# Where on one DMA queue the copy of x to the output goes out: two pieces early and six among the Toeplitz loads, instead of six early and two late

## The chip, the cores and the metric

The kernel runs on one core of one Trainium2 chip. The metric is the time of one execution in microseconds; the kernel before takes 540.82 us, the median of three runs (539.96 to 542.36). A core has five engines, each with its own instruction stream: TensorE (PE in the profile) multiplies matrices, VectorE (DVE), ScalarE (ACT) and GpSimd (POOL) work elementwise, and SyncE (SP) here does nothing but wait on semaphores and issue DMAs. DMAs that SP issues are one queue (q1), those of ACT another (q10), those of POOL a third (q0); all three are served by the same 16 DMA engines.

## The reference

x has the shape 32 x 64 x 1024 (batch, channel, time), all float32. The layer convolves each channel over time with a kernel of its own, then runs a mixture of experts over the 2048 (channel, batch) rows and adds its result to x:

```python
kernel = _get_kernel(log_dt, C, log_A_real, A_imag, Lq)      # 64 channels x 1024 taps
y = irfft(rfft(u*mask) * rfft(kernel))[..., :Lq]             # causal convolution over time
y = (y + u_m * D[:, None]) * mask
...
logits = y_rows @ gate_w.T ; top 2 of 16 experts, weights w
h = silu(y_rows @ g.T) * (y_rows @ u.T)                      # 112 wide per expert
out = einsum('bei,hei,be->bh', h, d_r, w)
return x + out.reshape(x.shape)
```

The "x +" of the last line is what this change is about: the output tensor has to hold a copy of x before the experts' results are added into it.

## The kernel before

**The convolution.** The 64 channels are worked in 16 groups of 4 (`G` = 16, `HG` = 4). A channel's convolution is a product with a Toeplitz matrix. For group g, TensorE makes the taps (`products`, k_bank), VectorE copies them out (`kernel_rows`, k_sb), SP stores them to a DRAM tensor `k_rows` (L303, 16 KB), and SP then reads them back as a Toeplitz matrix: 128 partitions, each one a row of 1024 taps that starts one element further (L314 for groups 0 and 1, four loads of 512 KB with a semaphore each; L317 for the others, one load of 2 MB). I call these the tap store and the Toeplitz load of a group. Also needed is the group's part of x with time on the partitions (`x_time`, L308, 512 KB). TensorE then runs 8 matmuls of up to 256 columns for each channel (L988; the trace counts 16 records for them), VectorE masks them (L742) and transposes blocks (L751), and ACT stores the group's rows to DRAM (`y_rows`, L525, four stores of 128 KB).

**What orders SP's queue.** `toep` and `u_t` have two buffers each, picked by g % 2. In each turn of its loop over g SP does this, in order: wait until the taps of g are in k_sb (`k_added`); issue the tap store; wait until the convolution of group g-2 has ended (`conv_done`); issue the load of x_time; wait until the tap store has landed (`k_stored`); issue the Toeplitz load of g. The next turn begins with the tap store of g+1. So the tap store of g+1 always stands behind the Toeplitz load of g in the same queue, and the Toeplitz load of g+1 is not issued before that store has landed.

**The copy of x.** `copy_x(q)` (L281 to L284) copies rows 256q to 256q+255 of x, 1 MB, from DRAM to DRAM, straight into `out`. There are eight pieces. Six are issued at the start, before the tap store of group 0; two are issued after the loop over g and after the weights of the first four experts (L296, L297). Only POOL waits for the pieces: `pool.wait_ge(x_copied, 8 * 16)`, ahead of the first scatter into `out`.

**The experts.** Rows are sorted by expert in tiles of 128. For each tile POOL gathers rows (L442), TensorE transposes them (L1105), multiplies with the gate and up weights (L1097) and the down weights (L1115), and POOL adds the weighted result into `out` by a scatter that accumulates (L458). Experts beyond the first four have their weights loaded as the earlier ones are used up.

Of the kernel before, what the change touches and what calls it, by code (L numbers as in the profile page):

```python
# [40 lines left out]
def build(nc, x_time, x_rows, lengths, params, skip, gate_t, gu_t, d_t, out):  # L41
# [4 lines left out]
    with ctx:  # L46
# [224 lines left out]
        @block.sync  # L271
        def _(sp):
            sp.dma_start(par[:, :, :], params).then_inc(par_in, 16)
            sp.dma_start(skip_row[:, :], skip).then_inc(par_in, 16)
            sp.dma_start(len_i[:, :], lengths.partition_broadcast(P)).then_inc(len_in, 16)
            sp.dma_start(gate_w[:, :, :], gate_t).then_inc(gate_in, 16)

            for g in range(2):
                sp.dma_start(u_t[:, g, :, :], x_time[:, g * HG:(g + 1) * HG, :]).then_inc(u_in[g], 16)

            def copy_x(q):  # L281

                part = slice(q * (TOK // 8), (q + 1) * (TOK // 8))
                sp.dma_start(out[part, :], x_rows[part, :]).then_inc(x_copied, 16)  # L284

            sp.wait_ge(ys_cleared, 1)
            sp.dma_start(out[TOK:, :], ys[:, 0, :]).then_inc(spare_out, 16)
            sp.wait_ge(zero_made, 1)
            sp.dma_start(k_rows.ap()[:, 0:P - 1], zero[:, 0:P - 1]).then_inc(pads_out, 16)
            for q in range(6):  # L290
                copy_x(q)
            sp.wait_ge(pads_out, 16)

            def load_expert(e):
                s = e % WB
                sp.dma_start(w_gu[:, s * C * GU:(s + 1) * C * GU], gu_t[e]).then_inc(w_in[s], 16)  # L296
                sp.dma_start(w_d[:, s * L:(s + 1) * L], d_t[e]).then_inc(w_in[s], 16)  # L297

            for g in range(G):
                p, i = g % 2, g // 2  # L300

                sp.wait_ge(k_added, g + 1)
                sp.dma_start(bass.AP(k_rows, g * HG * KROW + P - 1, [[LO, LO], [KROW, HG], [1, LO]]),  # L303
                             k_sb[:, p, :, :]).then_inc(k_stored[p], 16)

                if g >= 2:
                    sp.wait_ge(conv_done, (g - 1) * HG)
                    sp.dma_start(u_t[:, p, :, :], x_time[:, g * HG:(g + 1) * HG, :]).then_inc(u_in[p], 16)  # L308

                sp.wait_ge(k_stored[p], 16 * (i + 1))  # L310
                if g < 2:

                    for h in range(HG):
                        sp.dma_start(toep[:, p, h, :], bass.AP(k_rows, (g * HG + h) * KROW, [[1, P], [1, L]])  # L314
                                     ).then_inc(toep_first[p][h], 16)
                else:
                    sp.dma_start(toep[:, p, :, :], bass.AP(k_rows, g * HG * KROW, [[1, P], [KROW, HG], [1, L]])  # L317
                                 ).then_inc(toep_in[p], 16)

            for e in range(WB):  # L320
                load_expert(e)
            for q in range(6, 8):
                copy_x(q)

            for e in range(WB):
                sp.wait_ge(w_in[e % WB], 32)
                sp.sem_inc(weights_ready, 1)
            sp.wait_ge(ends_made, 1)
            sp.wait_ge(lists_made, 1)
            for e in range(WB, E):  # L330

                end = sp.value_load(ends_i[0:1, e - WB:e - WB + 1], min_val=1, max_val=MT)
                sp.wait_ge(down_done, end)
                load_expert(e)
                sp.wait_ge(w_in[e % WB], 32 * (e // WB + 1))
                sp.sem_inc(weights_ready, 1)
# [851 lines left out]
```

## Time and profile before

| | |
|---|---|
| median of three runs | 540.82 us (539.96 to 542.36) |
| the profiled execution | 542.34 us |
| its span | 540.5 us |
| PE busy | 457.0 us, 85% |
| weight loads (PEld) busy | 391.3 us, 72% |
| DVE, ACT, POOL busy | 38%, 18%, 32% |
| DMA moved | 119.94 MB, mean 222 GB/s |
| SP's queue q1 | 73.49 MB, 41.4% of 16 engines' span |

The execution lasts 542.34 us, of which the profile's span holds 540.5. The kernel has three stages: a prologue to about 33 us, in which parameters are worked out while the DMA engines copy; the convolution, to about 220 us; then routing (to about 250 us) and the experts. The busy shares are means over all three, so the question for each stage is which wait ends last in it. The chain of waits (part 4 of the page, and the chain in order of time) follows the work that ended last back to what released it. The queue's own instructions are seen in SP's timeline; a row of it gives the start and length of the issue, not of the transfer.

### The profile page before, as it was taken

To read this page: it belongs to the slowest core of one execution; us is meant where nothing else is said; L and a number is where in the kernel's file an instruction comes from. 1 tells how busy PE (TensorE), PEld (TensorE's weight loads), DVE (VectorE), ACT (ScalarE), POOL (GpSimd) and SP (SyncE) were. 2 spreads that over 40 slices of the span, in tenths; PEclk is the share of its full clock that TensorE was granted. 3 is DMA by queue.
4 is the path that set the end of the run, shared out by engine and by line. 5 is a ranking of instruction groups with operands and counts; after the bars stand their busy time and mean duration, and the time that the engine had idled before them with its cause. 6 is when DMAs were issued, how large, how long until landed. Compare 5 with 4: busy or idle time off the path is not lost.

```text
span 540.5 us, 9417 instructions
## 1 busy us (share of the span) xinstructions
PE 457.0 (85%) x2867; PEld 391.3 (72%) x2868; DVE 204.6 (38%) x560; ACT 99.1 (18%) x230; POOL 172.1 (32%) x215
## 2 busy tenths in 40 slices
PE   0479799999998998958899889899899798899881
PEld 0469798988888988857777667677677576677660
DVE  6914334533334325494233233232333223333321
ACT  3930000000000000200122122221222122222210
POOL 5244222233221100063144332353343334344331
PEclk9989899999999999968899999999999989999996
DMA  8958978788888889922278878989887968868553
GB/s 297 312 159 274 310 244 274 274 266 279 285 289 256 290 269 333 333 106 77 75 216 215 213 182 247 249 232 258 231 180 225 274 185 183 241 134 176 83 80 69
DMA packets 39466, 119.94 MB, mean 222 GB/s; under 512 B 7442, under 2 KB 15890, under 8 KB 39314
## 3 DMA queue, kind: packets, MB, share of 16 engines
q1 hardware_dynamic: 18418, 73.49, 41.4%
q0 software_dynamic: 11808, 37.76, 31.6%
q10 hardware_dynamic: 9216, 8.39, 4.6%
q8 instruction: 13, 0.21, 0.2%
q14 instruction: 11, 0.09, 0.1%
HBM read 94.68 MB, written 38.57 MB: 247 GB/s over the span
## 4 chain that ended last, share of the span: by engine, by line
PE 44%; DMA 35%; issue 8%; DVE 8%; POOL 2%; ACT 0%; POOLq 0%; ACTq 0%; DVEq 0%; SPq 0%
PE conv_ps L988 18%; DMA out<-od,to_row 12%; PE conv_ps L1097 11%; DMA ys<-y_rows,from_row 10%; DMA arena<-k_rows 7%; PE conv_ps L1115 7%; DMA k_rows<-k_sb 6%; PE turn_ps L1105 4%; PE conv_ps L1083 1%; PE turn_ps L999 1%; DVE tmp L637 1%; POOL out L458 1%; DVE od L933 1%; POOL arena L430 1%; DVE mask_t L786 1%
## 5 line engine op out<-in xcount | busy, mean ns | idle before, releaser
L988 PE MATMUL conv_ps<-arena 128*128 128x256 f32 (+7 forms) x1024 | 158.4, 311 | 16.5 <-DMA arena<-k_rows 9.6
L988 PEld LDWEIGHTS conv_ps<-arena 128*128 128x128 f32 x1024 | 150.3, 194 | 24.6 <-issue 13.5
L1097 PE MATMUL conv_ps<-w_gu,ys_t 128*128 x656 | 135.9, 361 | 13.8 <-issue 11.5
L1097 PEld LDWEIGHTS conv_ps<-w_gu,ys_t 128*128 128x128 f32 x656 | 122.3, 192 | 33.3 <-issue 32.9
L458 POOL DMA_INDIRECT out<-od,to_row x40 | 63.5, 1587 | 132.3 <-DMA out<-od,to_row 70.1
L1115 PE MATMUL conv_ps<-w_d,hid_t 112*128 x160 | 76.9, 603 | 0.0
L742 DVE TENSOR_TENSOR arena<-conv_ps,mask_t 128x256 f32<-128x256 f32 x64 | 26.9, 423 | 97.9 <-PE conv_ps L988 96.8
L442 POOL DMA_INDIRECT ys<-y_rows,from_row x42 | 44.5, 1059 | 46.4 <-PE turn_ps L1105 34.3
L933 DVE TENSOR_SCALAR od<-conv_ps,weight_now 128x512 f32<-128x512 f32 x40 | 30.0, 751 | 72.2 <-DMA out<-od,to_row 47.1
L1105 PE MATMUL turn_ps<-ident,ys 128*128 128x128 f32 x336 | 45.8, 281 | 13.3 <-DMA ys<-y_rows,from_row 13.3
L1105 PEld LDWEIGHTS turn_ps<-ident,ys 128*128 128x128 f32 x336 | 39.7, 144 | 18.5 <-DMA ys<-y_rows,from_row 17.0
L913 DVE TENSOR_TENSOR hid<-silu,conv_ps 128x112 f32<-128x112 f32 x41 | 11.1, 271 | 91.7 <-ACT silu L576 91.7
L387 POOL TENSOR_TENSOR am<-wave,cs_re 128x128 f32<-128x128 f32 x16 | 6.4, 399 | 117.1 <-ACT wave L519 109.6
L1115 PEld LDWEIGHTS conv_ps<-w_d,hid_t 112*128 112x128 f32 x160 | 27.7, 193 | 20.3 <-issue 19.8
L584 ACT ACTIVATE od<-conv_ps,weight_now 128x512 f32<-128x512 f32 x40 | 27.5, 687 | 75.1 <-DMA out<-od,to_row 48.2
L905 DVE COPY ys_t<-turn_ps 128x512 f32<-128x512 f32 x42 | 29.1, 692 | 27.7 <-PE turn_ps L1105 27.4
L569 ACT COPY ys_t<-turn_ps 128x512 f32<-128x512 f32 x42 | 24.6, 585 | 66.1 <-PE turn_ps L1105 65.5
L576 ACT ACTIVATE silu<-conv_ps 128x112 f32<-128x112 f32 x41 | 10.8, 262 | 96.2 <-PE conv_ps L1097 96.1
L519 ACT ACTIVATE wave<-angle 128x384 f32<-128x384 f32 x16 | 8.2, 521 | 106.7 <-DVE angle L687 106.7
L1039 PE MATMUL turn_ps<-ones 128*128 128x128 f32 x50 | 8.3, 341 | 20.7 <-DVE cs_im L722 20.7
L430 POOL TENSOR_TENSOR arena<-arena,token_no 128x384 f32<-128x384 f32 (+1 forms) x5 | 7.2, 1449 | 54.4 <-DVE arena L867 54.4
L1039 PEld LDWEIGHTS turn_ps<-ones 128*128 128x128 f32 x50 | 7.9, 251 | 20.4 <-issue 20.4
(151 smaller groups left out, 309.8 us busy)
## 6 DMA issues: line engine op xcount, KB each, us to landing
arena<-k_rows SPq DMA_DIRECT2D x14, 2048.0 KB, 10.9
w_gu<-gu_t SPq DMA_DIRECT2D x16, 896.0 KB
arena<-x_time SPq DMA_DIRECT2D x16, 512.0 KB, 4.0
y_rows<-y_blk ACTq DMA_DIRECT2D x64, 128.0 KB, 7.4
w_d<-d_t SPq DMA_DIRECT2D x16, 448.0 KB
arena<-k_rows SPq DMA_DIRECT2D x8, 512.0 KB, 6.0
ys<-y_rows,from_row POOLq DMA_INDIRECT x42
out<-od,to_row POOLq DMA_INDIRECT x40
```

Source lines behind the costliest of these rows:

```text
L442: nc.gpsimd.indirect_dma_start(out=ys[:, t % 2, :], out_offset=None, in_=y_rows, in_offset=bass.IndirectOffsetOnAxis(ap=from_row[:, t:t + ...
L458: nc.gpsimd.indirect_dma_start(out=out, out_offset=bass.IndirectOffsetOnAxis(ap=to_row[:, t:t + 1], axis=0), in_=od[:, t % 2, :], in_offse ...
L569: nc.scalar.copy(ys_t[:, p, 0:C // 2, :], ytr_ps[:, 0:L // 2].rearrange("p (c n) -> p c n", n=P)).then_inc(yst_act, 1)
L584: nc.scalar.mul(od[:, p, 0:L // 2], down_ps[:, 0, :], weight_now[:, p:p + 1]).then_inc(od_act, 1)
L742: nc.vector.tensor_tensor(y_t[:, p, h, :, :], conv_ps[:, h, 0:C * B].rearrange("p (c b) -> p c b", c=C), mask_t[:, :, :], ALU.mult).then_i ...
L905: nc.vector.tensor_copy(ys_t[:, p, C // 2:, :], ytr_ps[:, L // 2:].rearrange("p (c n) -> p c n", n=P)).then_inc(yst_dve, 1)
L933: nc.vector.tensor_scalar(od[:, p, L // 2:], down_ps[:, 1, :], weight_now[:, p:p + 1], None, ALU.mult, ALU.bypass).then_inc(od_dve, 1)
L988: last = nc.tensor.matmul(conv_ps[:, h, d * B:C * B], toep[:, p, h, d * P:(d + 1) * P], u_t[:, p, h, 0:(C - d) * B], start=(d == 0), stop= ...
L1039: nc.tensor.matmul(bank, ones[:, :], ones[:, :], start=True, stop=True)
L1097: last = nc.tensor.matmul(gu_ps, ys_t[:, p, c, :], w_gu[:, bass.ds(buf * (C * GU) + c * GU, GU)], start=(c == 0), stop=(c == C - 1))
L1105: last = nc.tensor.transpose(ytr_ps[:, c * P:(c + 1) * P], ys[:, p, c * P:(c + 1) * P], ident[:, :])
L1115: last = nc.tensor.matmul(down_ps[:, n, :], hid_t[:, p, :], w_d[:, bass.ds(buf * L + n * (L // 2), L // 2)], start=True, stop=True)
```

## The change

Two pieces of the copy are issued at the start instead of six. The other six are issued one at a time in the loop over g, each right behind the Toeplitz loads of groups 1, 3, 5, 7, 9 and 11. None is left behind the expert weights. All other instructions are the same, on all engines.

```diff
@@ -287,7 +287,7 @@
             sp.dma_start(out[TOK:, :], ys[:, 0, :]).then_inc(spare_out, 16)
             sp.wait_ge(zero_made, 1)
             sp.dma_start(k_rows.ap()[:, 0:P - 1], zero[:, 0:P - 1]).then_inc(pads_out, 16)
-            for q in range(6):
+            for q in range(2):
                 copy_x(q)
             sp.wait_ge(pads_out, 16)
 
@@ -316,11 +316,11 @@
                 else:
                     sp.dma_start(toep[:, p, :, :], bass.AP(k_rows, g * HG * KROW, [[1, P], [KROW, HG], [1, L]])
                                  ).then_inc(toep_in[p], 16)
+                if g in (1, 3, 5, 7, 9, 11):
+                    copy_x((1, 3, 5, 7, 9, 11).index(g) + 2)
 
             for e in range(WB):
                 load_expert(e)
-            for q in range(6, 8):
-                copy_x(q)
```

What SP issues from the start to the load of group 2, before and then after (`out<-x_rows` is a piece of the copy, `k_rows<-k_sb` a tap store, `arena<-k_rows` a Toeplitz load, `arena<-x_time` the group's part of x):

```order
L284 DMA out<-x_rows 16x16384 x6
L303 DMA k_rows<-k_sb 32x4x32
L314 DMA arena<-k_rows 128x1024 x4
L303 DMA k_rows<-k_sb 32x4x32
L314 DMA arena<-k_rows 128x1024 x4
L303 DMA k_rows<-k_sb 32x4x32
L308 DMA arena<-x_time 128x1024
L317 DMA arena<-k_rows 128x4x1024
```

```order
L284 DMA out<-x_rows 16x16384 x2
L303 DMA k_rows<-k_sb 32x4x32
L314 DMA arena<-k_rows 128x1024 x4
L303 DMA k_rows<-k_sb 32x4x32
L314 DMA arena<-k_rows 128x1024 x4
L284 DMA out<-x_rows 16x16384
L303 DMA k_rows<-k_sb 32x4x32
L308 DMA arena<-x_time 128x1024
L317 DMA arena<-k_rows 128x4x1024
```

Four pieces have left the place ahead of the first tap store, and one now stands between the Toeplitz loads of group 1 and the tap store of group 2.

Further on in the loop, SP's stream around the Toeplitz load of group 3, as a piece of the difference:

```order
 L308 DMA arena<-x_time 128x1024
 L317 DMA arena<-k_rows 128x4x1024
+L284 DMA out<-x_rows 16x16384
 L303 DMA k_rows<-k_sb 32x4x32
 L308 DMA arena<-x_time 128x1024
```

One piece stands ahead of the tap store of group 4; four more such places follow, ahead of the tap stores of groups 6, 8, 10 and 12.

## Rows read from the trace of the kernel before

**Rows 1.** The page: busy tenths in 40 slices of 13.5 us, and chain shares.

```profile
PEclk9989899999999999968899999999999989999996
DMA  8958978788888889922278878989887968868553
PE 44%; DMA 35%; issue 8%; DVE 8%; POOL 2%; ACT 0%; POOLq 0%; ACTq 0%; DVEq 0%; SPq 0%
```

**Rows 2.** Chain in order of time, prologue and first groups: start, us, what.

```profile
24.20 4.90 DMA k_rows<-k_sb
29.11 4.20 DMA arena<-k_rows
33.44 4.02 PE conv_ps L988 x16
...
46.25 2.46 PE conv_ps L988 x16
...
56.89 2.89 issue
59.78 3.95 PE conv_ps L988 x16
```

**Rows 3.** Chain in order of time, the middle of the convolution.

```profile
105.05 0.92 issue
...
108.11 9.29 DMA k_rows<-k_sb
117.42 11.03 DMA arena<-k_rows
```

**Rows 4.** SP's timeline, its DMA issues: start, us, line, DMA, count.

```profile
4.96 4.94 SPq L284 DMA_DIRECT2D out<-x_rows  x6
24.20 0.35 SPq L303 DMA_DIRECT2D k_rows<-k_sb  x1
...
38.36 0.32 SPq L303 DMA_DIRECT2D k_rows<-k_sb  x1
40.28 1.75 SPq L314 DMA_DIRECT2D arena<-k_rows  x4
...
71.67 0.33 SPq L308 DMA_DIRECT2D arena<-x_time  x1
72.05 0.43 SPq L317 DMA_DIRECT2D arena<-k_rows  x1
...
115.69 0.33 SPq L308 DMA_DIRECT2D arena<-x_time  x1
117.42 0.37 SPq L317 DMA_DIRECT2D arena<-k_rows  x1
...
197.03 0.37 SPq L317 DMA_DIRECT2D arena<-k_rows  x1
```

**Rows 5.** Windows: stretch, length, engines' busy us, PE clock, DMA share, GB/s.

```profile
11.00:14.00 3.00, 0.00 (x0) 0.00 (x0) 2.71 (x6) 2.95 (x9) 2.33 (x5) 1.00 1.02 350
14.00:17.00 3.00, 0.00 (x0) 0.00 (x0) 2.62 (x12) 2.99 (x9) 0.00 (x0) 1.00 1.05 371
17.00:20.00 3.00, 0.00 (x0) 0.00 (x0) 2.76 (x17) 3.00 (x14) 0.00 (x0) 1.00 1.07 350
20.00:23.00 3.00, 2.09 (x9) 1.82 (x10) 2.93 (x13) 3.00 (x14) 2.17 (x6) 1.00 1.04 328
23.00:26.00 3.00, 3.00 (x19) 2.94 (x20) 2.90 (x7) 3.00 (x14) 0.69 (x1) 1.00 1.14 355
26.00:29.00 3.00, 3.00 (x28) 3.00 (x27) 0.95 (x3) 2.98 (x13) 0.00 (x0) 1.00 0.04 6
72.00:197.00 125.00, 117.17 (x985) 110.75 (x985) 51.80 (x120) 8.15 (x21) 27.05 (x58) 1.00 0.86 279
```

**Rows 6.** Timeline of PE, ACT and POOL where the convolution begins.

```profile
23.53 6.30 PE L1039 MATMUL turn_ps<-ones 128*128 128x128 f32 x42
32.35 0.45 POOL L396 TENSOR_TENSOR am<-am,arena 128x128 f32<-128x128 f32 x1
37.39 0.44 PE L980 MATMUL k_bank<-bm,am 128*32 128x32 f32 x8
```

**Rows 7.** Timeline of PE, first and last channels of groups: start, us, idle time before.

```profile
105.36 2.48 PE L988 MATMUL conv_ps<-arena 128*128 128x256 f32 x16 [0.70 <-DMA arena<-k_rows]
108.35 4.79 PE L988 MATMUL conv_ps<-arena 128*128 128x256 f32 x32
113.19 2.46 PE L988 MATMUL conv_ps<-arena 128*128 128x256 f32 x16
117.09 2.48 PE L988 MATMUL conv_ps<-arena 128*128 128x256 f32 x16 [1.07 <-DMA arena<-k_rows]
...
209.00 2.46 PE L988 MATMUL conv_ps<-arena 128*128 128x256 f32 x16 [2.10 <-issue]
```

**Rows 8.** Chain in order of time behind the convolution, to the first gather.

```profile
240.16 7.81 PE conv_ps L1083 x48
...
249.65 5.38 DMA ys<-y_rows,from_row
```

**Rows 9.** Windows around the two late pieces, columns as in rows 5.

```profile
203.00:233.00 30.00, 24.79 (x210) 23.47 (x208) 17.03 (x90) 3.83 (x7) 0.00 (x0) 1.00 1.03 332
229.00:240.00 11.00, 5.50 (x33) 5.09 (x31) 10.63 (x24) 0.53 (x2) 5.97 (x6) 0.75 0.35 138
```

**Rows 10.** Tile x_rows, issue to landing of the eight pieces; tile out, POOL's scatters.

```profile
DMA to landing us min/median/max: 8.7/16.6/30.2
...
L458 POOL DMA_INDIRECT out<-od,to_row x40: 1552/1587/1631, 273.0 to 530.6; - x40
```

## The prediction

> **What bounds the kernel now.** I read the page first. Its slices of 13.5 us show the DMA engines busy for seven to nine tenths through the whole convolution, slices 4 to 15, and the chain that ended last is PE for 44% and DMA for 35% [rows 1]. So in that stage two things are near their limit, and the question is which wait ends last in each group.
>
> The chain in order of time answers it. In the middle of the convolution it goes from a tap store, 9.29 us from issue to landing, straight to a Toeplitz load, 11.03 us [rows 3]. The same 16 KB store takes 40.28 - 38.36 = 1.92 us when the queue ahead of it is empty [rows 4]. So the other 7.4 us are the Toeplitz load of the group before, which stands ahead of it in SP's queue. PE started on that load's data at 117.09 [rows 7] and the store landed by 117.42, when SP issued the next load [rows 4]. Each group therefore costs one full pass of the queue: Toeplitz load, tap store behind it, receipt, next Toeplitz load. From 72.05 to 197.03 there are 11 groups [rows 4], 11.36 us each.
>
> PE is close behind but not the limit. A group's matmuls run from 105.36 to 113.19 + 2.46 = 115.65; PE's next group starts at 117.09, after 1.07 us without work that ended with the Toeplitz load [rows 7]. The last group starts at 209.00 after 2.10 us of idling [rows 7]. A group keeps PE busy for some 10.7 us, the 117.17 us busy over 11 groups [rows 5]. SP issues x_time at 115.69, when group g-2 has ended, 1.7 us ahead of the Toeplitz load [rows 4]; that loop has 1.7 us of slack.
>
> In the prologue the pieces of the copy run from before 11 us to 26 us, and from 26 to 29 the DMA engines carry next to nothing, 6 GB/s [rows 5]. The tap store of group 0 was issued at 24.20 and took 4.90 us [rows 2].
>
> **The start.** Two pieces instead of six end some 12 us earlier, at about 14 us, far ahead of the store at 24.20. The store then takes its 1.92 us instead of 4.90: 2.98 us less. It lands at 26.1, and the first Toeplitz channel 4.20 us later [rows 2], at 30.3. PE's filler matmuls end at 23.53 + 6.30 = 29.8 [rows 6], so its idle time falls from 3.6 us to about 0.6. The first 16 matmuls took 4.02 us after the long idling, where a warm group's take 2.46 [rows 2]; I expect 2.46, another 1.5 us. What is late next is POOL: the factors of group 1 are ready at 32.35 + 0.45 = 32.8, and PE's products of group 1, now at 37.39, come at 30.4 + 2.5 = 32.9 [rows 6]. That just fits. Sum for the start: -4.5 us. Bounds: -3.0 if the first channel stays slow, -4.5 if not.
>
> **The six moved pieces.** A piece is 256 rows of 4 KB, 1.05 MB. In the five windows from 11 to 26 us the queue moves 350, 371, 350, 328 and 355 GB/s for 3 us each [rows 5], 5.26 MB in 15 us, so 3.0 us a piece. In the changed program each stands behind a Toeplitz load and ahead of the next tap store. The store waits for the queue to drain, as its 9.29 us show, so its landing and the next Toeplitz load move by the whole piece. Nothing hides it: the engines' idle time of the stage, 14% [rows 5], 1.6 us of each 11.36, lies behind the tap store, while its receipt comes back and the next load is issued, and a piece ahead of the store can't slide there. Six times 3.0 is +18.0 us. The issue itself, 4.94 / 6 = 0.8 us on SP [rows 4], is over before the load ahead of it has drained. An upper bound for a piece comes from the mean rate of the stage, 279 GB/s [rows 5], at which 1.05 MB take 3.8 us, 22.5 us for six.
>
> Two small terms go the other way. The Toeplitz load of group 4 was issued at 72.05 only because group 2's matmuls ended late: x_time went out at 71.67 [rows 4], since PE had idled 2.89 us and run a slow first channel of 3.95 us [rows 2]. With a piece in front of that load, PE is no longer what it waits for; I take 0.5 us off. And as every pair of groups gets 3 us longer, x_time and the y_rows stores are issued earlier against the Toeplitz load and fill more of the idle 1.6 us. That lies between 0 and 6 x 1.6 = 9.6 us. I take 2.0, close to nothing, because x_time already goes out 1.7 us ahead and its 0.5 MB take about that long.
>
> PE waits for each even group some 3 us longer. Behind its waiting matmul are the gates and products of that turn, and VectorE and ACT wait for these; all of them have two groups of room. After 2.89 us of idling PE's first channel took 3.95 us instead of 2.46 [rows 2]. So 1.5 us more for PE every second group; a pair then takes it 2 x 10.7 + 1.5 = 22.9 us against 2 x 11.36 + 3.0 = 25.7 us of queue. It stays hidden.
>
> **The two late pieces.** They leave the stretch 203 to 233 us, where DMA runs at 332 GB/s [rows 9]. Nothing on the chain waits for them: it goes through routing to the 48 table matmuls at 240.16 and the gather at 249.65, which takes 5.38 us [rows 8], and by 229 to 240 the DMA rate has fallen to 138 GB/s [rows 9]. POOL needs the copy first at its scatter at 273.0 [rows 10]. Gain 0. The new last piece, behind group 11, lands by about 165 us, so no wait is added there either. The weights of the first experts still follow the last Toeplitz load and move with it.
>
> **Sum.** -4.5 + 18.0 - 0.5 - 2.0 = +11.0 us. The profiled execution took 542.34 us (span 540.5), so 553.3 for it. It lay 1.5 us above the median of the runs; against the median that is 551.8, say 552.
>
> **A rule that speaks against the change even more.** The copy moved 351 GB/s in the prologue, which counts each byte once; read and written it is some 700 GB/s at the DRAM [rows 5]. The Trainium skill, page "HBM Reference", section "Specifications (TRN2)", puts a core's effective share of the memory's bandwidth at about 358 GB/s. By that, 2.1 MB read and written for a piece would take an estimated 5.9 us, and six of them 35 us. This case's trace doesn't agree for a copy that runs by itself, at 3.0 us a piece.
>
> **The rivals.**
>
> 1. The pieces are hidden (faster). If the store did not wait for them, because the engines took it past the piece or spread the piece over their idle time, six pieces would need 18 us of a stage in which 14% of 125 us, 17.5 us, are idle [rows 5]. Cost about 0, and the start's 4.5 us stay: 536.3 us. For it: the room is just enough. Against it: the 9.29 us of the store show that it is served behind what is ahead of it. It decides as soon as the tap store behind a piece lands no later than one without. 7%.
>
> 2. Part of it is hidden. The idle time is filled to between half and all: 4.8 to 9.6 us back instead of 2, so +3.4 to +8.2, 544 to 549 us, centre 546. 13%.
>
> 3. Reading and writing at once is the limit beside other traffic. In the stage the memory already serves 279 GB/s, and a piece has to be read and written. At 279 GB/s for both ways together a piece costs 2 x 3.8 = 7.5 us, six 45, with the start +40: 581 us. The windows of 700 GB/s both ways speak against it, though there nothing else ran. 2%.
>
> 4. PE's slow clock comes onto the path, or the pieces cost the 3.8 us. If each of six idle times brings 1.5 us that are not hidden, +9 on top of 11: 561 us; with 3.8 us a piece and nothing filled, 22.5 - 3.0 = +19.5, 560 us. For it: 2.89 us of idling did bring the slow channel. Against: the 2.8 us of room for a pair. 9%.
>
> **How the numbers follow.** The forecast, +7 to +16 us, 548 to 557, gets 69%. The range takes in the second rival and the upper bound of the fourth, 544 to 560, and leaves out the hidden copy and the memory limit. Within 0.5% (2.7 us, about what a measurement of this kernel can tell from no change) lies the edge between rivals 1 and 2, 5%; faster by more 6%; slower by more 89%.
>
> **What would show it.** In the changed profile: the tap store of group 0 lands about 2 us after its issue, and the first matmul on Toeplitz data starts near 30.5 us. SP's Toeplitz issues alternate, about 14.2 us from odd to even groups and 11.3 from even to odd, up to group 12, then 11.4 steadily. PE waits some 3 us for the Toeplitz load of each even group. The last group's matmuls start near 220 us instead of 209.00, and what follows keeps its length. The forecast is wrong if the steps from odd to even groups stay near 11.4 us, or if the copy costs over 4 us a piece.

## The result and the profile after

The changed kernel takes 548.12 us (median of four, 546.38 to 553.12) against 540.39 of the kernel before in the same series: ratio 1.0152, 95% interval 1.008 to 1.0225. It is slower by some 8 us, as forecast in sign; the forecast was 552.0, the range 544 to 560. Some executions of every kernel run in a slower state with a lower clock: the ratios leave them out, the medians given here and below are of all executions.

The profiled execution is a long one, 553.12 us with a span of 551.3. The page's slices, columns as in [rows 1], show the emptied slice 2 (13.8 to 27.6 us) and a granted clock that fell to 0.6 and 0.7 in slices 5 and 9 (0.8 and 0.9 before), and more mildly in slice 12:

```profile
PEclk9999699979989999978799999999999989999996
DMA  8079968878999889901377879989887978767753
```

SP's timeline of the changed kernel answers to [rows 4]:

```profile
24.21 0.35 SPq L303 DMA_DIRECT2D k_rows<-k_sb  x1
25.76 1.77 SPq L314 DMA_DIRECT2D arena<-k_rows  x4
...
36.04 1.75 SPq L314 DMA_DIRECT2D arena<-k_rows  x4
37.83 0.62 SPq L284 DMA_DIRECT2D out<-x_rows  x1
...
47.63 0.38 SPq L317 DMA_DIRECT2D arena<-k_rows  x1
...
57.36 0.37 SPq L317 DMA_DIRECT2D arena<-k_rows  x1
57.77 0.56 SPq L284 DMA_DIRECT2D out<-x_rows  x1
...
72.09 0.34 SPq L308 DMA_DIRECT2D arena<-x_time  x1
72.48 0.43 SPq L317 DMA_DIRECT2D arena<-k_rows  x1
...
84.64 0.37 SPq L317 DMA_DIRECT2D arena<-k_rows  x1
...
98.37 0.37 SPq L317 DMA_DIRECT2D arena<-k_rows  x1
...
109.07 0.37 SPq L317 DMA_DIRECT2D arena<-k_rows  x1
...
123.30 0.34 SPq L308 DMA_DIRECT2D arena<-x_time  x1
123.69 0.43 SPq L317 DMA_DIRECT2D arena<-k_rows  x1
...
180.96 0.43 SPq L317 DMA_DIRECT2D arena<-k_rows  x1
```

The first store lands 1.55 us after its issue. I call the time from one group's Toeplitz issue to the next group's a step. The steps alternate, as foreseen: from group 5 (84.64) to 6 it is 13.7 us, from 6 to 7 10.7. Over the six of each kind from group 1 to 13, the steps from odd to even groups average 13.5 us (before: 11.1) and those from even to odd 10.6 (before: 11.4). At groups 4 and 8 something else shows: x_time went out 0.39 us ahead of the Toeplitz load. There SP was not waiting for the tap store but for PE, which had to end groups 2 and 6 (at group 4 the trace of before shows the same, 71.67 and 72.05 in [rows 4]). PE's timeline shows why (start, length, idle time ahead; the columns of [rows 7]):

```profile
57.25 4.66 PE L988 MATMUL conv_ps<-arena 128*128 128x256 f32 x16 [4.45 <-issue]
62.85 6.69 PE L988 MATMUL conv_ps<-arena 128*128 128x256 f32 x32
...
108.43 4.69 PE L988 MATMUL conv_ps<-arena 128*128 128x256 f32 x16 [2.32 <-DMA arena<-k_rows]
114.06 6.68 PE L988 MATMUL conv_ps<-arena 128*128 128x256 f32 x32
...
158.06 3.86 PE L988 MATMUL conv_ps<-arena 128*128 128x256 f32 x16 [2.64 <-DMA arena<-k_rows]
162.64 4.79 PE L988 MATMUL conv_ps<-arena 128*128 128x256 f32 x32
```

Behind its waits PE ran at 0.50 of its clock, the lower of its two levels (1.2 instead of 2.4 GHz), in the windows from 57 to 66 and from 108 to 117 us, and groups 2 and 6 took some 4.5 us longer each than the groups behind them. Group 10 lost 1.4 us.

The last group's channels start at 214.84 instead of 209.00 [rows 7], +5.8 us; the first gather comes at 256.24 instead of 249.65 [rows 8]. From there to the end of the span it is 295.1 us against 290.9, 4.2 us that come behind the loop.

### The profile page after: what moved, and what is told of

Its sections match the earlier page's. It is cut to its first block, busy times and chain, and to the rows that moved or that the text cites. A ratio compares the mean times of both kernels' runs of the same rounds, so it can differ in the third digit from the quotient of the medians.

```text
span 551.3 us, 9417 instructions
## 1 busy us (share of the span) xinstructions
PE 465.9 (85%) x2867; PEld 396.4 (72%) x2868; DVE 205.1 (37%) x560; ACT 99.2 (18%) x230; POOL 172.4 (31%) x215
## 4 chain that ended last, share of the span: by engine, by line
DMA 39%; PE 38%; issue 7%; DVE 5%; ACT 4%; POOL 3%; POOLq 1%; ACTq 0%; DVEq 0%; SPq 0%
DMA out<-od,to_row 23%; PE conv_ps L988 22%; DMA ys<-y_rows,from_row 8%; PE conv_ps L1097 6%; PE conv_ps L1115 4%; DMA k_rows<-k_sb 4%; DMA arena<-k_rows 4%; ACT arena L503 3%; PE turn_ps L1105 3%; PE turn_ps L999 1%; PE conv_ps L1083 1%; DVE od L933 1%; POOL ys L442 1%; POOL out L458 1%; POOL arena L430 1%
## 5 line engine op out<-in xcount | busy, mean ns | idle before, releaser
L988 PE MATMUL conv_ps<-arena 128*128 128x256 f32 (+7 forms) x1024 | 165.0, 320 | 14.8 <-issue 7.3
L988 PEld LDWEIGHTS conv_ps<-arena 128*128 128x128 f32 x1024 | 156.3, 201 | 23.4 <-issue 17.9
L1115 PE MATMUL conv_ps<-w_d,hid_t 112*128 x160 | 78.2, 612 | 0.0
L913 DVE TENSOR_TENSOR hid<-silu,conv_ps 128x112 f32<-128x112 f32 x41 | 11.1, 272 | 90.8 <-ACT silu L576 90.8
L1115 PEld LDWEIGHTS conv_ps<-w_d,hid_t 112*128 112x128 f32 x160 | 27.6, 193 | 20.9 <-issue 19.7
L576 ACT ACTIVATE silu<-conv_ps 128x112 f32<-128x112 f32 x41 | 10.8, 263 | 95.5 <-PE conv_ps L1097 95.3
## 6 DMA issues: line engine op xcount, KB each, us to landing
y_rows<-y_blk ACTq DMA_DIRECT2D x64, 128.0 KB, 7.0
w_d<-d_t SPq DMA_DIRECT2D x16, 448.0 KB, 11.7
```

What stands on the lines that cost most here:

```text
L988: last = nc.tensor.matmul(conv_ps[:, h, d * B:C * B], toep[:, p, h, d * P:(d + 1) * P], u_t[:, p, h, 0:(C - d) * B], start=(d == 0), stop= ...
L1115: last = nc.tensor.matmul(down_ps[:, n, :], hid_t[:, p, :], w_d[:, bass.ds(buf * L + n * (L // 2), L // 2)], start=True, stop=True)
```

## The experiments

All were timed in five rounds beside the kernel before: e1 to e4 together, e5 to e8, e9 and e10, e11 and e12. For each I also give, from its trace, the time from the Toeplitz issue of group 1 to that of group 13, "the twelve steps". It holds the six pieces and leaves out the start. In the first trace of before it is 175.01 (the row below) less 40.28 [rows 4], 134.7 us; in that of the changed kernel 180.96 - 36.04 = 144.9.

```profile
175.01 0.37 SPq L317 DMA_DIRECT2D arena<-k_rows  x1
```

| kernel | ratio to before (95%) | median us, all executions | twelve steps |
|---|---|---|---|
| changed | 1.0152 (1.008 to 1.0225) | 548.12 | 144.9 |
| e6 changed, again | 1.019 (1.0119 to 1.0261) | 545.31 | 139.5 |
| e5 before, again | 1.0005 (0.9956 to 1.0053) | 538.23 | 129.2 |
| e1 five early, three late | 0.9957 (0.9923 to 0.999) | 534.52 | 129.2 |
| e7 two early, six late | 0.9926 (0.988 to 0.9973) | 533.14 | 132.1 |
| e12 the same, PE warmed | 0.9914 (0.9874 to 0.9955) | 531.85 | 128.0 |
| e4 pieces behind tap stores | 1.003 (0.9989 to 1.0072) | 539.52 | 135.9 |
| e3 fillers at even groups | 1.0159 (1.0118 to 1.02) | 545.19 | 141.7 |
| e8 pieces on ACT's queue | 1.0151 (1.008 to 1.0222) | 545.70 | 144.2 |
| e9 six extra pieces | 1.0149 (1.0073 to 1.0225) | 547.26 | 143.6 |
| e2 twelve halves | 1.0241 (1.0197 to 1.0284) | 550.47 | 144.4 |
| e10 three pairs | 1.0258 (1.0206 to 1.031) | 550.58 | 152.1 |
| e11 three pairs, PE warmed | 1.014 (1.0087 to 1.0193) | 543.14 | 138.5 |

**e1, five pieces early, three late.**

```diff
-            for q in range(6):
+            for q in range(5):
...
-            for q in range(6, 8):
+            for q in range(5, 8):
```

> Five pieces go out at the start and three behind the expert weights; none in the loop over the groups. Theory A (the start's gain is real, the moved pieces are the loss): the fifth piece ends at about 23 us, before the tap store of group 0 at 24.2, so the store lands in under 2 us, the convolution starts near 29.8 us and ends 3 to 4.5 us earlier than in the kernel before, at 215.5 to 217 us; 536 to 537.5 us in all. Theory B (what starts earlier is lost again at a later wait): the convolution ends at 219 to 220 us and the time is 540 to 541.

Measured: the first Toeplitz load was issued at 25.71 (before: 29.11 [rows 2] and 28.55), the ratio is 0.9957. The start's gain is real, some 2.3 us by the ratio (0.5 to 4.1 by its interval). The trace ended its convolution at 208.3, earlier than A said, because its steps from group 6 on were 10.3 to 10.9 us long and not 11.4. That called for a second trace of before (e5).

**e2, twelve halves.**

```diff
-                if g in (1, 3, 5, 7, 9, 11):
-                    copy_x((1, 3, 5, 7, 9, 11).index(g) + 2)
+                if 1 <= g <= 12:
+                    half = slice((g + 3) * (TOK // 16), (g + 4) * (TOK // 16))
+                    sp.dma_start(out[half, :], x_rows[half, :]).then_inc(x_copied, 16)
```

> Two pieces early as in the changed kernel; the other 6 MB go out as twelve halves, one behind the Toeplitz load of each group from 1 to 12. Same bytes in the same stage. Theory A (PE's slow clock behind its long waits costs some 4 us each at groups 2 and 6): each wait of PE is 1 to 2 us, the granted clock stays at 1.00 after group 2, and the time falls to 543 to 545 us. Theory B (only the bytes in SP's queue count, the clock is hidden): 548 us as in the changed kernel.

Measured: 1.0241. A fails. The slow channels did not vanish (4.1, 4.2 and 4.0 us at groups 2, 5 and 12), and the steps average 12.0 us. B said no change; it came out higher than the changed kernel, though the intervals overlap, so that halves cost more is not shown. In this trace no step from group 2 on is shorter than 10.7 us, where the changed kernel's steps behind a long one are 9.7 to 10.8 in five of six cases.

**e3, fillers on TensorE at even groups.**

```diff
+            def convolve(g, p, i, second=False, warm=0):
+                if warm:
+                    pe.wait_ge(conv_read, g * HG - HG + 1)
+                    stay_awake(warm, conv_ps[:, 0, 0:P])
...
+                    convolve(2 * i + p, p, i, False, 8 * (1 - p))
```

> The changed kernel with 8 more filler matmuls (128x128, about 2.3 us) on TensorE ahead of each even group from 2 to 12, where it waits for the Toeplitz load. Theory A (slow clock costs): the clock stays at 1.00 from group 2 on, the matmuls of groups 2 and 6 take 2.5 us for the first channel instead of 4.7, the Toeplitz issues alternate all the way (about 13.5 and 10.2 us), and the convolution ends 2 to 5 us earlier than in the changed kernel: 543 to 546 us. Theory B (the queue alone): the convolution ends where it did or later by what fillers are not hidden: 548 to 552 us.

Measured: 1.0159, the same as the changed kernel's 1.0152 and 1.019. In its trace the steps alternate all the way (13.2 and 10.4 us on average), and the only slow channel ahead of the last group is 3.9 us at group 2. The twelve steps, 141.7, lie between the two traces of the changed kernel. The 545.19 us lie in A's range only because the kernel before was shorter in this series (537.96). So no gain of the fillers shows; the intervals (1.0118 to 1.02 against 1.0119 to 1.0261 for e6) leave room for one of a few us.

**e4, the pieces right behind the tap stores.**

```diff
                              k_sb[:, p, :, :]).then_inc(k_stored[p], 16)
+                if g in (2, 4, 6, 8, 10, 12):
+                    copy_x(g // 2 + 1)
...
-                if g in (1, 3, 5, 7, 9, 11):
-                    copy_x((1, 3, 5, 7, 9, 11).index(g) + 2)
```

> The six pieces go out right behind the tap stores of groups 2, 4, ..., 12 instead of right ahead of them, so the store's receipt no longer waits for the piece but the Toeplitz load does. Theory A (a piece ahead of the store can't fill the idle gap of the queue, one behind it can): each step from an odd to an even group is 1 to 1.5 us shorter than in the changed kernel, and PE's waits too; 541 to 545 us. Theory B (bytes count, place doesn't): 548 us.

Measured: 1.003, against 1.0152 for the same pieces one place earlier in the queue. A holds in kind, and by more than it said: the steps from odd to even groups average 11.15 us, 1.6 to 2.4 less than in the two traces of the changed kernel. B is excluded. SP's timeline around the piece of group 6 (issue times; "landing" below is from the answers for one issue each):

```profile
81.25 0.37 SPq L319 DMA_DIRECT2D arena<-k_rows  x1
83.97 0.32 SPq L303 DMA_DIRECT2D k_rows<-k_sb  x1
84.34 0.53 SPq L284 DMA_DIRECT2D out<-x_rows  x1
91.27 0.33 SPq L310 DMA_DIRECT2D arena<-x_time  x1
92.27 0.37 SPq L319 DMA_DIRECT2D arena<-k_rows  x1
```

The Toeplitz load of 81.25 lands after 10.5 us, the store by 92.27, and the next load goes out at once: a step of 11.0 us with a piece in it. The piece lands at 94.5, while the load's own data are on their way. In the changed kernel the step with the same piece was 13.7 us.

**e5 and e6, both kernels again.** No edit.

> The kernel before, unchanged, for a second trace of it beside a second one of the changed kernel. In its first trace the Toeplitz issues of groups 4 to 15 came 11.36 us apart; in the trace with five pieces early they came 10.6 us apart, which is PE's pace, though the loop is the same. Theory A (the queue pass of 11.4 us is the loop's own): 11.3 to 11.5 us here too, the last group's convolution ends at 218 to 220 us. Theory B (two paces are possible for the same loop, and the start decides): some stretch of groups at 10.5 to 10.7 us here, an end before 216 us.

> The changed kernel, unchanged, on the same chip as the others of this group. Theory A (its stage behind the convolution is no longer than before; the first profiled execution was merely a long one): median 7 to 8 us above the kernel before, the convolution ends at 224 to 226 us, and the gather comes 30.5 to 31 us behind that. Theory B (the change lengthens the experts' stage): the time from the first gather to the end is 3 to 4 us longer than in the kernel before in this trace too.

Measured: for e5 B holds in its steps, though its convolution ends no earlier than 215.6 us because the last load took 13.3 us; its profiled execution, 542.07 us, is one of its longer ones, so I read only its steps, which agree with e1's. SP's timeline of e5 has steps of 11.7 and 11.5 us up to 93.24 and then 10.4 to 10.8, PE's pace:

```profile
81.71 0.37 SPq L317 DMA_DIRECT2D arena<-k_rows  x1
...
93.24 0.37 SPq L317 DMA_DIRECT2D arena<-k_rows  x1
...
103.26 0.33 SPq L308 DMA_DIRECT2D arena<-x_time  x1
103.94 0.37 SPq L317 DMA_DIRECT2D arena<-k_rows  x1
...
113.91 0.33 SPq L308 DMA_DIRECT2D arena<-x_time  x1
114.35 0.38 SPq L317 DMA_DIRECT2D arena<-k_rows  x1
```

From group 7 to 14 x_time goes out 0.37 to 0.68 us ahead of the Toeplitz load, where the first trace has 1.5 to 1.8 in most of these groups: here SP's last wait is mostly the one for PE and no longer the one for the tap store. e1 shows the same from group 7 on.

For e6 the median is 6.7 us above before, and the ratio of 1.019 means some 10 us, 6.4 to 14 by its interval, which holds A's 7 to 8. Its trace (span 541.2 us) has the gather 31.5 us behind the convolution and 291.2 us from there to the end: A for the experts' stage. Its convolution ended at 218.5, earlier than A said: here too the loop is faster than in the first traces. Groups 2, 6 and 10 ran slow first channels, 4.1, 3.9 and 4.1 us, but the second and third at full speed, and at group 4 SP waited for the store, not for PE. The windows over groups 2 and 6 in the first trace and in e6 (columns of [rows 5]) show the granted clock:

```profile
56.00:70.00 14.00, 12.75 (x68) 11.73 (x69) 1.43 (x4) 0.50 (x2) 2.86 (x6) 0.63 0.84 296
107.00:121.00 14.00, 12.57 (x67) 11.55 (x68) 3.37 (x10) 0.79 (x2) 2.85 (x6) 0.63 0.90 314
```

```profile
56.00:70.00 14.00, 13.01 (x94) 12.36 (x95) 2.33 (x6) 0.51 (x2) 2.86 (x6) 0.88 0.86 289
107.00:121.00 14.00, 14.00 (x122) 13.16 (x121) 4.52 (x10) 0.30 (x2) 2.35 (x5) 0.94 0.91 305
```

The difference of the twelve steps is the same in both pairs of traces, changed minus before: 144.9 - 134.7 = 10.2 and 139.5 - 129.2 = 10.3 us. That they agree so well is luck. The first trace of the changed kernel is 5.5 us longer than e6, 4.7 of them in the steps from group 3 to 4 and from 7 to 8, where SP waited for the slow PE (15.12 and 14.62 us against 12.62 and 12.42); the first trace of before is 5.6 us longer than e5, because it kept the slower pace. Crosswise, the differences would be 4.7 and 15.8 us. SP's timeline of e6 at group 8, where it waited for the store, is:

```profile
106.06 0.37 SPq L317 DMA_DIRECT2D arena<-k_rows  x1
...
117.54 0.34 SPq L308 DMA_DIRECT2D arena<-x_time  x1
118.48 0.37 SPq L317 DMA_DIRECT2D arena<-k_rows  x1
```

**e7, two early, six late.**

```diff
-            for q in range(6):
+            for q in range(2):
...
-            for q in range(6, 8):
+            for q in range(2, 8):
```

> Two pieces early, none in the loop, six behind the expert weights of the first four experts. Theory A (the late pieces are free as long as they land before the first scatter): as with five early, 0.3 to 0.9% below the kernel before. Six pieces behind the weights end at about 239 us, so the gather at about 245 us isn't touched. Theory B (late pieces cost, by the y_rows stores or the gathers that run beside them): 2 to 4 us above the kernel with five early.

Measured: 0.9926, below before. Six pieces behind the weights cost nothing that shows, with the first gather at 241.5 in this trace. A holds. e7 and the changed kernel have the same start and differ in nothing but the place of the six pieces, so they give the price of the places most directly: 1.019 - 0.9926 in this series, 14 us, and with the 1.0152 of the first series 12 us; 2.0 to 2.4 us a piece. Taken the same way, e4's place costs 1.003 - 0.9926, 5.6 us or 0.9 a piece.

**e8, the pieces on ACT's queue.**

```diff
             def rows_out(g, p, piece=None):
...
+                if piece is not None:
+                    part = bass.ds(piece * (TOK // 8), TOK // 8)
+                    act.dma_start(out[part, :], x_rows[part, :]).then_inc(x_copied, 16)
```

> The six pieces go out on ACT's queue, each behind the y_rows stores of groups 1, 3, 5, 7, 9 and 11, at about the time at which the changed kernel issues them on SP's. Same bytes, same stage, but no tap store stands behind a piece. Theory A (a piece costs because the tap store behind it in the queue has to wait until it has drained, so it can't use the gap): 1 to 1.5 us a piece, as behind the tap stores, 538 to 543 us on a chip where the kernel before takes 540. Theory B (the 16 engines are what is full, the queue doesn't matter): as the changed kernel, 547 to 549.

Measured: 1.0151, beside 1.019 for the changed kernel in the same series. B holds. The profiled execution, 551.50 us, is one of its two long ones, so only one load is read from it. Its queues around one piece:

```profile
80.27 0.37 SPq L317 DMA_DIRECT2D arena<-k_rows  x1
81.39 0.32 SPq L303 DMA_DIRECT2D k_rows<-k_sb  x1
84.11 0.66 ACTq L527 DMA_DIRECT2D out<-x_rows  x1
90.26 0.33 SPq L308 DMA_DIRECT2D arena<-x_time  x1
93.50 0.37 SPq L317 DMA_DIRECT2D arena<-k_rows  x1
```

Nothing stands ahead of the tap store but the load, yet the load of 80.27 took 12.7 us to land and the step is 13.2. So the order in SP's queue is not what the piece costs here. My reading, which fits e4 and e8 but was not tested by itself, is that a piece beside the load takes the engines' time from it as one behind it does, and that e4's is cheap because it runs while the store's receipt comes back and the next load starts.

**e9, six extra pieces.** e1, with six more pieces at the changed kernel's places that copy x to a DRAM tensor of their own.

```diff
+        aside = nc.dram_tensor("aside", [TOK, L], fp32).ap()
...
+                if g in (1, 3, 5, 7, 9, 11):
+                    part = slice((g // 2) * (TOK // 8), (g // 2 + 1) * (TOK // 8))
+                    sp.dma_start(aside[part, :], x_rows[part, :]).then_inc(x_copied, 16)
```

> The kernel with five pieces early and three late, with six more pieces of 1 MB in the loop at the changed kernel's places, which copy x to a DRAM tensor that nothing reads: the price of the six places by itself, with the start and the late pieces as in the kernel with five early. Theory A (the places are the loss, about 1.7 us each, 10 us between the Toeplitz issues of groups 1 and 13): those issues are 139 to 145 us apart instead of 129, and the time is 7 to 11 us above that of the kernel with five early, so 5 to 9 us above the kernel before. Theory B (a piece costs its whole 2.6 to 3 us and the changed kernel got some of it back by having no pieces behind the weights): 14 to 18 us above five early, 12 to 16 above the kernel before.

Measured: 1.0149. Against e1, 1.0149 - 0.9957 = 0.0192 of 537 us, 10.3 us for six places, 1.7 each (from two series, so by their ratios; the intervals allow 1.0 to 2.5 each). That is A's value; the lower end of B's is just inside the interval. That late pieces cost nothing is shown by e7 rather than by this.

**e10, three pairs of pieces; e11, the same with PE kept warm.**

```diff
-                if g in (1, 3, 5, 7, 9, 11):
-                    copy_x((1, 3, 5, 7, 9, 11).index(g) + 2)
+                if g in (1, 5, 9):
+                    copy_x(g // 2 + 2)
+                    copy_x(g // 2 + 3)
```

```diff
-            convolve(2, 0, 1, True)
+            convolve(2, 0, 1, True, 24)
...
+                    convolve(4 * j + g, g % 2, 2 * j + g // 2, False, 16 if g == 2 else 0)
```

> The changed kernel with its six pieces in three pairs, behind the Toeplitz loads of groups 1, 5 and 9. Same bytes; the halves cost more than the whole pieces. Theory A (each long pass of the queue is followed by one that is some 1 us short, because x_time and the y_rows stores have gone ahead of it, so fewer long passes give less back): 3 x 5.2 - 3 x 1 = 12.6 us from six pieces, 548 to 552 us on a chip where the kernel before takes 539, and PE's slow clock after waits of 5 us on top. Theory B (the more the bytes are gathered, the cheaper): 540 to 544 us.

> The six pieces in three pairs behind groups 1, 5 and 9, and 24, 16 and 16 filler matmuls (128x128, 0.29 us each at the high clock) on TensorE ahead of the Toeplitz waits of groups 2, 6 and 10. Theory A (in the kernel with pairs, PE's slow clock after each long wait is on the path: the first channel takes some 4.7 us and the second and third 6.7, 4 us a time, and the Toeplitz load of two groups later waits for it): the clock stays at 1.00, steps of 12.8 to 15.2 us between Toeplitz issues at groups 3 to 4, 7 to 8 and 11 to 12 shrink to 10.5 to 12, the issues of groups 1 and 13 come 140 to 145 us apart instead of 152, and the time is 1.005 to 1.015 of the kernel before instead of 1.026. Theory B (the clock is hidden, the bytes are the loss): 1.02 to 1.03.

Measured: 1.0258 for e10 (A), 1.014 for e11 (A). In e11 TensorE's loop is also unrolled to four groups a turn, to place the fillers; no run has that alone. PE's timeline at group 6, first in e10, then in e11 (L1043 are the fillers):

```profile
110.99 4.69 PE L989 MATMUL conv_ps<-arena 128*128 128x256 f32 x16 [3.69 <-DMA arena<-k_rows]
116.62 6.68 PE L989 MATMUL conv_ps<-arena 128*128 128x256 f32 x32
```

```profile
102.22 3.84 PE L1043 MATMUL conv_ps<-ones 128*128 128x128 f32 x32
106.47 2.46 PE L989 MATMUL conv_ps<-arena 128*128 128x256 f32 x16 [0.42 <-issue]
109.44 4.79 PE L989 MATMUL conv_ps<-arena 128*128 128x256 f32 x32
```

With the fillers the twelve steps fall from 152.1 to 138.5 us: the steps at groups 3 to 4, 7 to 8 and 11 to 12 from 12.8, 15.2 and 15.1 to 10.6 each. Here, with waits of 7.6, 3.7 and 4.4 us in e10, PE's slow clock is on the path and costs 2.2 to 4.6 us a time. By the ratios it is 0.0118, some 6 us; the profiled execution of e10, 557.43, is the longest of its six.

**e12, e7 with PE warmed ahead of group 2.** 9 fillers there (`convolve(2, 0, 1, True, 9)`).

> Two pieces early, six behind the expert weights, none in the loop, and 9 filler matmuls (2.6 us) on TensorE ahead of group 2, where it waits 2.3 us and then runs its first channel in 4.1 us instead of 2.5. Theory A (this slow channel is on the path, since the Toeplitz load of group 4 waits for group 2): the load of group 4 is issued 1.5 us earlier and the time is 0.986 to 0.993 of the kernel before. Theory B (given back at the queue, whose pass of 11 us is the limit there): the same as without, 0.9926 within its interval.

Measured: 0.9914 against 0.9926 for e7, inside each other's intervals. The trace has what A says: group 2's first channel takes 2.5 us and the step from group 3 to 4 is 10.3 instead of 12.0. That it shortens the whole is not shown. Its median is the lowest of the study; like e7, it is faster than both kernels.

## Why the prediction came out as it did

**The bound** was read right for the trace it was read from: the queue's pass, with PE close behind. What one trace could not show is that 11.36 us a group is not fixed. The same loop ran at 11.4 throughout in one trace and at 10.4 to 10.8 from group 6 on in the other, 5.6 us over twelve steps, and there "PE is close behind but not the limit" is wrong: SP waited for PE last (e5, e1). Why the load then lands in about 10.1 us instead of 10.9 stays open.

**The start**, -4.5 us: right in kind. The Toeplitz issue of group 1 moved from 40.28 to 36.04, -4.2, with the first channel at 2.5 us and the products waiting for POOL, as worked out. In the second pair of traces it is 38.25 to 36.00, -2.3, mainly because that trace of before already had a first channel of 2.5 us. The ratio of e1 says 2.3 and that of e7, which also moves the other early pieces, 4.0; both intervals hold both values.

**The six pieces**, +18.0 us less 2.0 for filled gaps: right in mechanism, mis-sized. This is the step that put the forecast too high, by 4 us in the first series. By steps in the first pair, the odd-to-even ones grew by 2.5 us each and not 3.0 (the 0.5 us for group 4 included), and the even-to-odd ones shrank by 0.8 each; in the second pair it is +2.05 and -0.3. The sum is 10.2 and 10.3 us, where I had 15.5, and the changed kernel's side of the 10.2 holds 4.7 us of waiting for the slow PE, which the forecast put at nothing. By ratio, changed kernel against e7, it is 12 to 14 us. A piece landed 2.4 to 2.7 us behind the Toeplitz load in four of five cases, so it costs less than the 3.0 of the prologue; the rest is gap filling, which I put at 2.0 us, "close to nothing". Its sign is in the steps behind a piece: x_time went out 3.8 and 3.6 us ahead of the loads of groups 6 and 10, and these landed in 9.9 and 9.8 us, where those of before, groups 4 to 12, took 10.5 to 11.1. The upper end that I named for it, 9.6 us, was the better hint, and the second rival, partly hidden, the nearest to what came in the first series: 544 to 549 us.

**No store could slide past a piece**: right. In the first trace of the changed kernel the stores of groups 4 to 12 landed 0.2 to 0.8 us behind the piece ahead of them, and e4, with the pieces behind the stores, costs less. But the reason was too narrow. I argued by the order in SP's queue; e8, with the pieces in another queue, costs as much. So what counts seems to be when the piece uses the engines.

**PE's clock "stays hidden"**: wrong in the first trace. I allowed 1.5 us for a wait; groups 2 and 6 lost some 4.5 us each, and SP's loads of groups 4 and 8 waited for PE (x_time 0.39 us ahead instead of 1.7). In e6 it was 1.4 to 1.7 us and mostly hidden, which fits that no gain of the fillers shows (e3). That removing it shortens the run is shown only for the longer waits of the pairs (e10 against e11). The fourth rival had the right mechanism; here it came together with cheaper pieces.

**The late pieces**, 0: right (e7, e9).

**The Trainium skill's figure** ("HBM Reference", "Specifications (TRN2)") would have made a piece cost 5.9 us. The same section gives the 358 GB/s as each core's share with both cores of a pair streaming and puts a core alone well above it, and here one core runs, so the rule did not fit this case. Beside other traffic, which the prologue could not test, the steps with a piece grew by 2.05 to 2.5 us, so this case's traces don't agree with 5.9 us there either.

**The experts' stage** was to keep its length. In the profiled execution it is 4.2 us longer, in e6 0.4 us longer than in the first trace of before; over all traces it lies between 288 and 295 us, 288.2 to 292.6 in those of kernels without pieces in the loop and 288.5 to 295.1 in those with them. Its 4.2 us are luck for the forecast: the profiled execution was put at 553.3 us and took 553.12, though the last group's channels started at 214.84 and not near 220.

## What to carry to other kernels

A transfer that nobody waits for still has a place: ask what lands behind it, and put it where the queue waits for a receipt or where no load is behind it, not between a load and the small store that the next load waits for. The same megabyte cost 1.7 (e9) to 2.4 us (e7 against the changed kernel) there, about 1 us one place later (e4), and nothing that showed after the last load (e7). A wait that is added to TensorE can be paid twice when the clock falls behind it, so compare its room with a slow group, not with a slow channel.

## What the runs showed of the hardware

- The clock after a wait did not follow from its length: 2.32 us of idling were followed by 9 us at 0.50 (first trace of the changed kernel, group 6), 2.64 by a first channel of 3.86 us, and 2.10 us in [rows 7] by none.
- A 16 KB store to DRAM landed in 1.5 us when issued at 24.2 us behind two or five pieces that had gone out at the start (12 traces of eleven kernels), in 4.9 and 4.3 us behind six (the two traces of before), and in 1.9 to 2.3 us for group 1.
- The same 6 MB came out at 1.0241 as twelve halves and at 1.0152 and 1.019 as six pieces, with intervals that overlap, and, with PE kept warm, at 1.014 as three pairs and 1.0159 as six pieces (e3).
